# A GNN and expert-FFN block on one core: expert outputs sent out and gathered back by DMA, and weight chunks laid out as runs of 8 KB

## The reference, cut to what matters

```python
probs = softmax(xf @ gate_w.T + gate_b)               # 625 x 8
topw, topi = top_k(probs, 2)                          # two experts for each row
wm = where(routed, w_te, -1.0)
sel_w, sel_idx = top_k(wm.T, cap)                     # cap = 93 rows for each expert, by weight
sel_w = maximum(sel_w, 0.0)
xg = xf[sel_idx]
h = gelu(einsum('ecd,edh->ech', xg, w1) + b1)         # 512 -> 2048
out = einsum('ech,ehd->ecd', h, w2) + b2              # 2048 -> 512
of = zeros((T, D)).at[sel_idx.reshape(-1)].add((out * sel_w[..., None]).reshape(-1, D))
x = x + of
```

## Time and profile before

| | us |
|---|---|
| median of 3 runs | 2184.42 (2179.93 to 2185.44) |
| profiled execution, its own time | 2186.39 |
| profiled execution, its span | 2184.4 |
| expert stage, first `dispatch` matmuls to the last of them | 208.9 to about 436 |
| TensorE busy over the span | 2119.4 (97%) |

### The profile page before, as it was taken

How to read it: one execution, slowest core, us unless ns; L and a number is a source line. 1 busy time by engine, 2 the same in 40 slices (tenths; PEclk the granted TensorE clock), 3 DMA queues, 4 the chain that set the end, 5 groups by cost and what they waited for, 6 DMA issues and landing times.

```text
span 2184.4 us, 36235 instructions
## 1 busy us (share of the span) xinstructions
PE 2119.4 (97%) x13402; PEld 1973.2 (90%) x13402; DVE 1507.6 (69%) x3184; ACT 1123.4 (51%) x3011; POOL 854.6 (39%) x687
## 2 busy tenths in 40 slices
PE   8887999999899999999999999999999999999998
PEld 7766666669779999999999999999999999999997
DVE  8736978864357776676767766777676777767676
ACT  4534656641455554455555445555544555555454
POOL 0000000000145555455555545555554555555461
PEclk9888999999989999999999999999999999999999
DMA  6000888870021321111122111112211111221110
GB/s 212 1 20 11 259 271 278 275 260 6 9 82 62 102 84 62 62 62 62 63 98 88 62 62 62 62 62 90 96 63 62 63 62 62 83 101 65 59 44 24
DMA packets 85688, 197.44 MB, mean 90 GB/s; under 512 B 5937, under 2 KB 10321, under 8 KB 85511
## 3 DMA queue, kind: packets, MB, share of 16 engines
q1 hardware_dynamic: 85512, 195.12, 26.5%
HBM read 193.75 MB, written 1.35 MB: 89 GB/s over the span
## 4 chain that ended last, share of the span: by engine, by line
PE 89%; ACT 4%; DVE 3%; DMA 1%; issue 1%; SPq 0%; POOL 0%; DVEq 0%; ACTq 0%; POOLq 0%
PE PS L54 80%; PE PS L53 5%; PE PS L57 4%; ACT HW L88 1%; ACT GT L88 1%; DMA RAW<-in_L_ffn_w 1%; DMA X<-in_x 0%; SPq L123 0%; ACT HS L88 0%; DVE OHs L68 0%; POOL SM L60 0%; DVE SM L107 0%; ACT EE L88 0%; DVE JU L66 0%; DVE M L75 0%
## 5 line engine op out<-in xcount | busy, mean ns | idle before, releaser
L54 PE MATMUL PS<-ZH,WS 128*128 128x314 f32 x4096 | 946.4, 311 | 0.0
L54 PEld LDWEIGHTS PS<-ZH,WS 128*128 128x128 f32 x4096 | 692.2, 189 | 0.0
L54 PE MATMUL PS<-ZL,WS 128*128 128x314 f32 x2048 | 626.1, 306 | 0.0
L60 DVE TENSOR_TENSOR ACC<-ACC,PS 128x314 f32<-128x314 f32 x1008 | 476.6, 477 | 196.7 <-PE PS L54 186.8
L54 PEld LDWEIGHTS PS<-ZL,WS 128*128 128x128 f32 x2048 | 387.7, 189 | 0.0
L60 POOL TENSOR_TENSOR WS<-RAW,WS 128x512 fp32r<-128x512 f32 x256 | 326.1, 1295 | 117.0 <-ACT WS L88 117.0
L60 POOL TENSOR_TENSOR ZS<-ZS,ZQ 128x628 f32<-128x628 f32 x128 | 198.3, 1549 | 231.0 <-ACT ZQ L88 230.9
L60 POOL TENSOR_TENSOR ML<-MF,MH 128x400 fp32r<-128x400 f32 x124 | 130.6, 1053 | 364.7 <-ACT MH L88 364.7
L88 ACT ACTIVATE ZH<-PS,g1T 128x628 fp32r<-128x628 f32 x128 | 100.4, 785 | 313.8 <-PE PS L54 313.8
L88 ACT ACTIVATE EE<-EE,SM 125x100 f32<-125x100 f32 x640 | 233.0, 376 | 0.1
L88 ACT ACTIVATE MF<-PS 128x400 f32<-128x400 f32 x128 | 64.7, 505 | 315.9 <-PE PS L53 315.9
(11 more groups left out here) (338 smaller groups left out, 3739.0 us busy)
## 6 DMA issues: line engine op xcount, KB each, us to landing
RAW<-in_L_ffn_wz_w SPq DMA_DIRECT2D x66, 1024.0 KB, 6.2
RAW<-in_L_ffn_w SPq DMA_DIRECT2D x64, 1024.0 KB, 8.1
RAW<-in_L_ffn_Wq_w SPq DMA_DIRECT2D x32, 1024.0 KB, 8.4
CB<-c_rows SPq DMA_DIRECT2D x32, 195.3 KB
RAW<-in_L_gnn_W SPq DMA_DIRECT2D x4, 1024.0 KB, 8.7
RAW<-in_L_ffn_Wkv_w SPq DMA_DIRECT2D x4, 1024.0 KB, 5.2
RAW<-in_L_ffn_Wk_T SPq DMA_DIRECT2D x2, 1024.0 KB, 5.2
WB<-w_rows SPq DMA_DIRECT2D x6, 305.2 KB
```

The costliest lines, as they stand in the source:

```text
L54: return self.q.matmul(o, l, r, start=start, stop=stop)
L60: return Nothing() if self.q is None else self.q.tensor_tensor(out=o, in0=a, in1=b, op=op)
```

## The change

Three things are changed.

1. The outputs of experts 0 to 5 are no longer added by matmuls. ScalarE writes them as plain float32 (`OW`), SP's queue stores them to rows of a tensor in memory, `y_rows` (row 0 is zero, 94 rows for each expert), and DVE computes from the ranks, once, in expert 5 (`places`), which two rows of `y_rows` belong to each row of x (`IL`, `IH`). After `dispatch(7)` has read `XFH` and `XFL`, GpSimd issues ten indirect DMAs that gather these rows into the same place (`YL`, `YH`), and DVE adds them to X ahead of `scale(7)`. Experts 6 and 7 are as before. The transposes of `PO` and copies to `PT` are dropped for experts 0 to 5.
2. The host lays out each chunk so that a partition's 8 KB are contiguous.
3. `sp_pool` is issued ahead of the expert stage, behind the degrees of the first graph convolution.

```diff
+    def gather(self, dst, src, index):
+        if self.q is None:
+            return Nothing()
+        return self.q.indirect_dma_start(out=dst, out_offset=None, in_=src, in_offset=bass.IndirectOffsetOnAxis(ap=index, axis=0))
...
         def load(q, n):
-            k, src = slot_of(n), srcs[n]
-            dst = RAW[k][:, :, :] if src.shape[1] == 4 else RAW[k][:, :, :].rearrange("p a b -> p (a b)").rearrange("p (a b) -> p a b", a=src.shape[1])
-            return q.dma(dst, src).then_inc(s_raw[k], 16)
+            k = slot_of(n)
+            return q.dma(RAW[k][:, :, :].rearrange("p a b -> p (a b)"), srcs[n]).then_inc(s_raw[k], 16)
...
+        NB = 6
+        yrow = nc.dram_tensor("y_rows", (1 + NB * CS, D), f32, kind="Internal").ap()
...
+            def outputs(e):
+                q.wait_ge(*os_hi.of(e))
+                for lo, hi in ((0, 80), (80, CS)):
+                    q.dma(yrow[1 + CS * e + lo:1 + CS * e + hi, :], OW[lo:hi, e % 2, :]).then_inc(s_yw[e % 2], 16)
+
+            q.wait_ge(*deg_mm.of())
+            sp_pool(q)
...
-                if m == 8:
-                    sp_pool(q)
...
+                if m % 8 == 7 and m // 8 < NB:
+                    outputs(m // 8)
...
         def g_moe(q):
...
+            q.wait_ge(*code_v.of("low"))
+            q.wait_ge(s_rows, 16)
+            q.wait_ge(s_yw[0], 32 * 3)
+            q.wait_ge(s_yw[1], 32 * 3)
+            q.wait_ge(*ga_mm.of(NE - 1))
+            for Y, index in ((YL, IL), (YH, IH)):
+                for t in range(T5):
+                    q.gather(Y[:, t, :], yrow, index[:, t:t + 1]).then_inc(s_back, 16)
...
+            def back():
+                q.wait_ge(s_back, 16 * 2 * T5)
+                for name, Y in (("low", YL), ("high", YH)):
+                    for t in range(T5):
+                        q.wait_ge(*x2_done.of(NE - 2 if name == "low" else "low", t))
+                        q.tt(X[:, t, :], X[:, t, :], Y[:, t, :], ALU.add).then_inc(*x2_done.up(name, t))
...
                 if e == NE - 1:
                     v_counts(q)
+                    back()
                 scale(e)
...
                 up(e, 0)
-                if e:
-                    combine(e - 1)
+                if e == NE - 1:
+                    combine(NE - 2)
                 up(e, 1)
```

More of the change, by code:

```diff
@@ L1014, in program @@
         wrow = nc.dram_tensor("w_rows", (8, 625), f32, kind="Internal").ap()
+        NB = 6
+        yrow = nc.dram_tensor("y_rows", (1 + NB * CS, D), f32, kind="Internal").ap()
+        s_rows, s_back = sem("s_rows"), sem("s_back")
+        s_yw = [sem(f"s_yw{k}") for k in range(2)]
+        code_v = count("code_v")
         def moe_raw(m):
@@ L1357, in scale, with places, step, after_ @@
                 q.tt(OT[:, :], PS[0:CS, 2, :], B2[:, k, :], ALU.add).then_inc(*ot_v.up(e))
-                q.wait_ge(*os_hi.of(e))
-                q.stt(OSL[:, k, :], OT[:, :], sw[k][:, 2:3], OS[:, k, :].bitcast(f32), ALU.mult, ALU.subtract).then_inc(*os_lo.up(e))
+                if e >= NB:
+                    q.wait_ge(*os_hi.of(e))
+                    q.stt(OSL[:, k, :], OT[:, :], sw[k][:, 2:3], OS[:, k, :].bitcast(f32), ALU.mult, ALU.subtract).then_inc(*os_lo.up(e))
+            def places():
+                def step(i, name):
+                    return i.then_inc(*code_v.up(name))
+                def after_(*names):
+                    for n in names:
+                        q.wait_ge(*code_v.of(n))
+                ranks, chosen = RKA[:, 0:NB, :], WM[:, :, 0:NB].rearrange("p t e -> p e t")
+                for e in range(NB):
+                    q.wait_ge(*rank_v.of(e, "sum"))
+                step(q.ts(CD[0][:, :, :], ranks, float(CAP), None, ALU.is_lt), "fits")
+                step(q.stt(CD[1][:, :, :], ranks, 1.0, EO[:, :, :], ALU.add, ALU.add), "row")
+                after_("fits")
+                step(q.stt(CD[0][:, :, :], chosen, 0.0, CD[0][:, :, :], ALU.is_ge, ALU.mult), "kept")
+                after_("row", "kept")
+                step(q.stt(CD[2][:, :, :], CD[1][:, :, :], -1000.0, CD[0][:, :, :], ALU.add, ALU.mult), "below")
+                step(q.tt(CD[1][:, :, :], CD[1][:, :, :], CD[0][:, :, :], ALU.mult), "above")
+                after_("below")
+                step(q.reduce(LH[0][:, :], CD[2][:, :, :].rearrange("p e t -> p t e"), ALU.min), "min")
+                after_("above")
+                step(q.reduce(LH[1][:, :], CD[1][:, :, :].rearrange("p e t -> p t e"), ALU.max), "max")
+                after_("min", "max")
+                step(q.stt(LH[2][:, :], LH[0][:, :], 1000.0, LH[1][:, :], ALU.add, ALU.is_lt), "two")
+                step(q.cp(IH[:, :], LH[1][:, :]), "high")
+                after_("two")
+                step(q.stt(IL[:, :], LH[0][:, :], 1000.0, LH[2][:, :], ALU.add, ALU.mult), "low")
@@ L1466, in dispatch @@
                 q.wait_ge(*free[5])
[L1467 to L1471, removed]
+                if e >= NB:
+                    for t in range(T5):
+                        o = PS[0:CS, 4, P * t:P * t + P] if t < 4 else PS[0:CS, 5, 0:P]
+                        i = q.tr(o, PO2[:, k, t, :].bitcast(f32), ident[0:P, 0:P])
+                    i.then_inc(*pt_t.up(e))
+                    free[4] = free[5] = pt_done.of(e)
                 q.wait_ge(*free[7])
@@ L2753, with chunks @@
     arrays, aps = {}, {}
+    def chunks(name, a):
+        if name in _ROW_CHUNKS:
+            k = _ROW_CHUNKS[name]
+            return a.reshape(-1, k, 128, 2048 // k).transpose(0, 2, 1, 3).reshape(-1, 128, 2048)
+        if name in _COLUMN_CHUNKS:
+            return a.reshape(-1, 4, 128, 4, 512).transpose(0, 3, 2, 1, 4).reshape(-1, 128, 2048)
+        return a
     for name in _INS:
```

83 lines of the change are left out of this document (45 added, 38 removed).

## The result

The changed kernel takes 2195.39 us (median of 4 runs, 2195.13 to 2197.26) against 2182.18 of the kernel before in the same comparison (4 runs, 2179.62 to 2185.44): a ratio of 1.0058, 95% interval 1.0041 to 1.0074. It is slower by 0.6%, where 2171.2 was forecast. The profiled execution took 2195.13 with a span of 2193.4, 9.0 more than before.

A forecast was written before the change was run, and what follows sets the result against it. TensorE, 97% busy, was taken as the bound. Between marks 15.2 us gained, plus 0.93 in expert 0's dispatch, less 2.85 for the additions: 13.3 gained, median 2171.2 us stated, range 2167 to 2179.

The forecast's parts named there:

- the one on the gathers: End of the expert stage: ten issues of 1.17 us and one landing give 17 us, within 34.9 us, so hidden.
- The upper bound: Ten gathers one after another, each as long as a 1 MB chunk, 5.1 us: 51 us, 16 too late.
- the gathers are late: Rival, end of stage: gain gone at 4.8 us per gather, 0.3% slower from 5.5; chance 0.12, of which 0.04 slower.
- Combines: Experts 1 to 6: six combines removed at 2.53 us each, 15.2 us gained; new pace 29.39 us per expert.
- The clock: Stops at experts' marks: one 1.5 us dip put back; rival, a dip at each of five, 6 us lost, chance 0.13.
- The trade that the prediction costed at nothing: Transposes of PO dropped ahead of the wait for GT: 0 gained, the stop grows by about 0.5 to 1.3 us.
- Small loads and DMA's allowance: Moved loads gain 1.23 and 0.63 us in experts 1 and 2; allowance falls to 7.4, expert 1's chunk 1.9 late.
- the DMA becomes the bound: Rival, experts 2 to 4: each late by 1 to 2 us, 3 to 6 us lost, 2174 to 2177; chance 0.17.
- Dispatch of expert 0, 0.93: Transposes dropped in the dispatch of expert 0, where nothing is awaited behind them: 0.93 us gained.
- The additions, 2.85: Ten additions on DVE behind the gathers, 6.2 us, delay OSL to 478.0 and so combine(7): 2.85 us lost.
- The rule on GpSimd's and VectorE's shared ports: Gather issues: contention with VectorE might slow them; each might take 1.5 us before anything is late, sum kept at 1.17.

The follow-up runs named there:

- layout_pool: The kernel before with only the new chunk layout (8 KB runs) and the small pooling loads moved early, all combines on TensorE: 2180.05 us, ratio 0.9975.
- early_turns: early_back with the PO transposes and copies to PT kept for all experts, though nothing reads them in six: 2169.34 us, ratio 0.9936 to the kernel before.
- pool_only: The kernel before with only the small loads of the pooling stage moved ahead of the expert stage: 2181.33 us, ratio 0.9994.
- hold_loads: The changed kernel with SP's queue waiting for all ten gathers before the last six chunk loads: 2176.7 us, ratio 0.9963 to the kernel before.
- early_back: The changed kernel with SP's queue waiting for the gathers before any later stage's load, and the additions ahead of the counts' split: 2174.2 us.

## Why the prediction was wrong

The profiled execution was to take 2173.1 us and took 2195.13, 22.0 more. Of these, 16.7 are at the end of the stage (19.6 lost, 2.85 forecast), 5.4 between the marks (9.8 gained, 15.2 forecast) and 0.9 in the dispatch of expert 0; 0.7 come back behind `combine(7)`, and 0.3 lie between the executions' own times and their spans.

**The step that failed** is the one on the gathers: "ten of these and one landing give 17 us. I take that: hidden." The ten issues took 14.4 us from the start of the first to that of the last, near their price. The one landing was taken as if the last gather had the engines to itself, 5.1 us; it took 36.28. The upper bound that the prediction had worked out, 51 us, is close to the 50.7 measured, but by chance: it had the gathers one after another, each like a chunk. What happened was something that the step left out. How fast the gathers moved depended on the piece size of the loads beside them (33, 42 and 51 us with 2, 4 and 8 KB), and the change had just made that four times as large. The rival "the gathers are late" had the right place and price list: 5.07 us each, between its points 4.8 (gain gone) and 5.5 (slower by 0.3%), though the kernel is already slower by 0.6%, since the marks had gained less than the rival supposed. It had a chance of 0.12, which was too low: the row nearest to a gather of 256 KB under load was a chunk's landing beside other transfers, 9.9 or 10.0 us in the earlier trace rows, not an operation of GpSimd.

**Combines: right.** Removing them moves everything up: 29.42 and 29.44 where nothing else interferes, 29.39 forecast. Between layout_pool and early_turns, whose ends are alike, the marks span 9.9 us less, not 15.2. Their medians are 10.7 us apart. The missing 5.3 between the marks are late chunks (stops of 2.61, 1.01 and 2.06 instead of 0.8: 3.3 us) and the dip behind the first of them (1.6), with 0.4 in small differences.

**The clock: the mechanism right, its number too small.** One dip of 1.5 was put back; the marks of the changed kernel show three, behind 268.49, 300.63 and 331.93, of 2.6, 1.5 and 1.5 us. This is 4.1 of the 5.4 us by which the marks fall short of the forecast. The trade that the prediction costed at nothing, dropping transposes ahead of a wait that ends when it ended, was a loss: it made the stops 1.4 us long instead of 0.8, and early_turns, which does the useless work, has 3.1 us less between the marks.

**Small loads and DMA's allowance: right in expert 1, too small behind it.** SP's queue is free of small loads at 252 us, the deciding chunk of expert 1 landed after 9.61 (9.3 to 9.5 forecast), and the stop at 268.49 is 2.4 us above 0.8 (1.9 forecast). pool_only has the two terms of the moved loads to 0.03 us each. What the sum missed is that the new layout clears the same excess. From expert 2 on the deciding chunk was to land after about 7 us, within the allowed 7.4. Most stops show no late chunk; in the changed kernel that of expert 3 took 7.68, and in early_turns those of experts 1, 3 and 4 stand in the chain that ended last (start, us, what):

```profile
249.87 9.45 DMA RAW<-in_L_ffn_w
...
312.31 7.65 DMA RAW<-in_L_ffn_w
...
341.98 8.68 DMA RAW<-in_L_ffn_w
```

The last two cost 1.5 us of stops (1.01 and 2.06 instead of 0.8), so a small part of the rival "the DMA becomes the bound" came true.

**Dispatch of expert 0, 0.93: not shown.** In the changed kernel the first mark stands at 236.80, before at 236.81. The profiled executions of pool_only and layout_pool, alike until then but for the layout, have it at 231.99 and 236.68, with 0.97 and 0.80 of full speed granted from 205 to 215 us, so a term of one microsecond can't be read there.

**The additions, 2.85: mis-sized, 4.2.** hold_loads shows the later start (2.7 us) and then 1.5 more, since `combine(7)` and what follows run at the lower clock (0.51 of full speed granted from 465 to 471 us). early_back shows that it needn't cost anything: the cover was VectorE's idle 7.45 us ahead of the counts, which the order of the additions left unused. It could be read before the change, in the same timeline as the earlier trace rows:

```profile
465.92 3.71 DVE L60 TENSOR_TENSOR gCL<-CT,gCH 125x628 fp32r<-125x628 f32 x5 [7.45 <-ACT gCH L88]
```

The rule on GpSimd's and VectorE's shared ports (the Trainium skill, SBUF — State Buffer, "Who interferes with whom") decided nothing here: the ten issues took 1.21 to 1.52 us each with VectorE busy for 9.9 of those 15.6 us, close to the 1.17 of the sum, and all were out 35 us before the last one landed.

## What to carry to other kernels

Two queues that shared the DMA engines here got about as many packets each (926 to 932, 626 to 627), not as many bytes: before adding a transfer of small pieces with a deadline, look which loads run beside it and how large their pieces are, and hold those that aren't needed yet; one wait on the loading queue turned 0.6% slower into 0.4% faster. A gather's cost was its landing beside that traffic, 36.28 us, not its issue of 1.2 to 1.5. And a stop of TensorE can cost more than its length: in these traces a stop of 0.8 to 1.0 us cost its own length, and one of 1.36 or more was followed by half clock in 30 of 41 cases, so that work dropped ahead of a wait can lose time. Last, look for idle time of the engine that gets new work before choosing its place: the ten additions cost 4.2 us behind the counts and nothing ahead of them.

## What was not expected of the hardware

A transfer written as four 2 KB pieces that are neighbours in memory goes out as 8 KB pieces: 39009 packets either way. Ten indirect gathers of 625 rows twice, 2.56 MB, moved at 55 GB/s beside loads of 8 KB pieces and at 174 GB/s nearly alone, less than half of a chunk load's 410, and each indirect gather needs GpSimd for 1.2 to 1.5 us, with 0.3 between two. Of the gathers' 2240 packets 1590 carry next to nothing, and most of the others two rows. Beside 8 KB pieces q0 got more packets than q1 (528 to 392); why it isn't one for one there as with 2 and 4 KB stays open.
